# Fixed PSUM banks for queries, score blocks and values in the second attention layer of a two-layer kernel

## The chip, the cores and the metric

The kernel runs on one core of one Trainium2 chip, in one launch. The metric is the device time in microseconds (us) of one execution, as the median of several. A core has five engines that work in parallel, each through its own queue, in order: TensorE (PE in the profile, its weight loads PEld), VectorE (DVE), ScalarE (ACT), GpSimd (POOL) and SyncE (SP), which issues transfers. They meet through semaphores. Matmul results land in PSUM, eight banks of 128 partitions by 512 float32 values, from which only DVE and ACT read.

## What is computed

Two layers on x of shape (8, 512, 128). Layer 1 is windowed attention and a top-1 mixture of experts. Layer 2, in which the change lies, is causal attention with one shared key and value head, and a gated feed-forward:

```python
xn = _layernorm(x, axis=-1)
x = x + _L1_attn_ref(xn, ...) + _L1_ffn_ref(xn, ...)
# _L1_attn_ref: 16 heads of 64, one k and v for all
xn = layernorm(x, g1)
q = xn @ Wq.T
kv = xn @ Wkv.T
k, v = (kv[..., :DIM_HEAD], kv[..., DIM_HEAD:])
q, k = (l2norm(q), l2norm(k))
q, k = (q * srt, k * srt)
sim = jnp.einsum('bhid,bjd->bhij', q, k)
sim = jnp.where(causal_mask, max_neg, sim)
attn = jax.nn.softmax(sim.astype(jnp.float32), axis=-1).astype(sim.dtype)
out = jnp.einsum('bhij,bjd->bhid', attn, v)
out = out @ Wout.T
return layernorm(out, g2)
# _L1_ffn_ref, weights dequantised from integers
h = jax.nn.silu(gate) * up
return jnp.einsum('bsh,dh->bsd', h, wd)
```

## The kernel before

Three stages run one after the other: layer 1's attention, the experts, then layer 2. Layer 2 runs one sequence b of 512 tokens after the other, `attend(b, last)`, seven in a loop and the eighth written out behind it. Each engine has its own `attend`; the order on an engine is the order of the code.

Within a sequence the 16 heads go in eight pairs, n = 0 to 7 (NP = 8). Two heads of 64 fill the 128 rows of the array side by side. For a pair:

- `project_q(n + 2)` on PE multiplies x by a slice of the query weights (ring_d<-wq_sb in the trace). `squares` on ACT squares the result (arena<-ring_d), `q_sums` on DVE sums it per head (q_sum), `q_length` on POOL takes the power (q_len), and `q_unit` on DVE scales, inverts and writes the normalised query into one of two buffers (q_nat_sb, o_n). q_unit frees the bank of the projected query.
- `turn_q(n + 1)` on PE transposes a normalised query. `q_turned` on ACT copies it twice, in full and rounded (arena, then rows), and `q_low` on DVE takes the difference. The semaphore q_lo then lets the scores of that pair go.
- `scores(n)` and `late_scores(n)` on PE form the scores by key block j = 0 to 3, of 512, 384, 256 and 128 queries (the causal mask cuts the rest), for both heads: three matmuls for each, since keys and queries are split in a high and a low part. `exp_of(n, third)` on ACT takes the exponential in three instructions: head 0 blocks 0 and 1, head 1 blocks 0 and 1, and blocks 2 and 3 of both.
- POOL cuts the diagonals (four selects), behind `q_length` of the same pair. `values1(n - 1)` on PE multiplies by v, and DVE's `values_out` copies the result out. Every second pair `sums1` adds the softmax sums of two pairs into the bank gather.

Between them run the three chunks of the feed-forward: `gate_up(c)` on PE (ring_a<-q_rows,w_gu), its emptying on ACT (tanh and a copy, xn_all<-ring_a), and `silu_up(c)` on DVE. Chunk 0 stands ahead of pair 0, chunks 1 and 2 behind the turn of q in pairs 0 and 1.

Seven of the eight banks are held by two rings. Ring D has three single banks (ring_d) and takes in turn projected queries, values, and at the end the feed-forward output and the spread sums. Ring A has two double banks (ring_a) and takes in turn both early thirds of the scores, the late third, the turned query and the gate/up chunks. A fill of a ring waits until its slot's last content was read. Ring R, for the start of the next sequence, uses the same banks as ring A. DVE also prepares the next sequence's rows in pairs 3 to 6.

## Time and profile before

| | |
|---|---|
| median of 3 runs | 1378.53 us (1378.07 to 1380.86) |
| the profiled execution | 1379.98 us, of which the span is 1378.1 us |
| busy in the span | PE 90%, DVE 65%, ACT 49%, POOL 33% |
| mean granted clock of PE | 0.96 |
| layer 2, all eight sequences | about 699 us |

The span goes from the first to the last instruction of one execution. A window's row gives the busy time of each engine in a stretch. In the order of time each row is an instruction or a run of equal ones, with its start, its length, and in brackets how long its engine was idle before it and what released it. The ends of matmuls are modelled and overlap by up to 0.1 us, so from one matmul group to the next it is best to subtract starts.

### The profile page before, as it was taken

The page shows a single profiled execution, that of the slowest core. Times are in us where ns is not written, and L with a number is a line of the kernel's source. Part 1 is how long each engine was busy: PE and PEld are TensorE (multiplying, and loading weights), DVE is VectorE, ACT ScalarE, POOL GpSimd, SP SyncE. Part 2 cuts the span into 40 slices and gives each one's busy share as a digit, 9 for nine tenths or more (in the row PEclk, how much of TensorE's full clock was granted, in tenths as well). Part 3 has the DMA queues.
Part 4 walks back from the last instruction along what each step waited for, and adds up shares of the span by engine and source line. Part 5 has one row for each costly group of instructions (what it writes and reads, how often), then busy time and mean ns, then how long its engine had stood idle before and what let it go on. Part 6 is the DMA issues. An engine that isn't in the chain of part 4 may idle for free.

```text
span 1378.1 us, 27031 instructions
## 1 busy us (share of the span) xinstructions
PE 1233.6 (90%) x8812; PEld 852.6 (62%) x8812; DVE 898.6 (65%) x2474; ACT 679.7 (49%) x1294; POOL 459.6 (33%) x695
## 2 busy tenths in 40 slices
PE   5999999999999958996499898998999989899896
PEld 3656656666566537996356656666576565656655
DVE  6888888888888754442465656556565566655644
ACT  2766667666766622442253543535425354353440
POOL 4221222212222245331263442534426245263340
PEclk9999999999999967998699999999999999999998
DMA  2300100001000052111000000000000000000000
GB/s 75 89 16 17 24 17 21 20 16 24 16 20 21 9 163 71 46 46 32 3 9 2 11 4 8 8 0 11 4 8 8 0 11 4 0 15 0 8 2 8
DMA packets 34597, 29.78 MB, mean 22 GB/s; under 512 B 5984, under 2 KB 27104, under 8 KB 34528
## 3 DMA queue, kind: packets, MB, share of 16 engines
q1 hardware_dynamic: 32224, 24.22, 6.5%
q0 software_dynamic: 2304, 4.72, 1.5%
q8 instruction: 34, 0.56, 0.2%
q14 instruction: 35, 0.29, 0.1%
HBM read 13.72 MB, written 6.82 MB: 15 GB/s over the span
## 4 chain that ended last, share of the span: by engine, by line
PE 34%; issue 9%; ACT 5%; DVE 2%; POOL 2%; POOLq 0%; ACTq 0%; DVEq 0%
PE ring_a L465 13%; PE ring_d L465 12%; PE gather L465 7%; ACT arena L1400 3%; PE ring_a L469 2%; ACT xn_all L1380 1%; POOL q_len L1163 1%; POOL klen L1169 0%; DVE k_rows L1844 0%; DVE arena L1916 0%; ACT k_rows L1339 0%; ACT arena L1372 0%; DVE m_cols L1902 0%; POOL arena L1187 0%; DVE q_rn L1780 0%
## 5 line engine op out<-in xcount | busy, mean ns | idle before, releaser
L1255 ACT ACTIVATE arena<-ring_a 128x384 f32<-128x384 f32 (+1 forms) x512 | 252.6, 550 | 138.9 <-PE ring_a L465 138.8
L1400 ACT ACTIVATE arena<-ring_a 128x896 f32<-128x896 f32 (+1 forms) x192 | 163.2, 884 | 206.9 <-PE ring_a L465 206.8
L1531 DVE CUSTOM_DVE_ANT_0 arena<-ring_d,arena 128x512 bf16<-128x512 f32 (+1 forms) x391 | 231.4, 614 | 37.5 <-PE ring_d L465 31.2
L1027 POOL TENSOR_SCALAR_AFFINE_SELECT arena<-arena 128x512 f32<-128x512 f32 x128 | 81.7, 639 | 357.1 <-ACT arena L1255 357.1
L465 PE MATMUL ring_a<-rows,k_rows 64*128 64x512 f32 (+3 forms) x1536 | 160.5, 343 | 43.8 <-ACT xn_all L1380 26.4
L465 PE MATMUL ring_a<-q_max,rows 128*128 128x384 f32 (+1 forms) x512 | 195.5, 385 | 0.9 <-ACT arena L1255 0.4
L465 PEld LDWEIGHTS ring_a<-rows,k_rows 64*128 64x128 f32 x1536 | 121.1, 192 | 81.4 <-ACT xn_all L1380 29.3
L465 PE MATMUL ring_d<-rows,q_rows 128*128 128x512 f32 (+1 forms) x391 | 161.3, 414 | 5.4 <-DVE mx L1531 3.3
L1163 POOL TENSOR_TENSOR q_len<-q_sum,exponents 128x8 f32<-128x8 f32 x64 | 105.2, 1645 | 182.0 <-DVE q_sum L1820 182.0
L465 PE MATMUL ring_d<-arena,v_aug 128*64 128x512 f32 (+3 forms) x1024 | 150.2, 438 | 0.0
L465 PEld LDWEIGHTS ring_d<-rows,q_rows 128*128 128x128 f32 x391 | 74.7, 191 | 81.5 <-DVE mx L1531 52.7
L465 PE MATMUL ring_a<-arena,v_aug 128*32 128x384 f32 (+1 forms) x1024 | 122.8, 551 | 1.9 <-POOL arena L1027 1.0
L465 PEld LDWEIGHTS ring_d<-arena,v_aug 128*64 128x64 f32 x1024 | 68.0, 136 | 78.9 <-issue 68.5
L1187 POOL TENSOR_SCALAR_AFFINE_SELECT arena<-arena 128x256 f32<-128x256 f32 x256 | 98.1, 413 | 42.9 <-ACT arena L1400 42.9
L1820 DVE TENSOR_REDUCE q_sum<-arena 128x8 f32<-128x512 f32 x64 | 43.7, 683 | 102.6 <-ACT arena L1372 102.6
L465 PEld LDWEIGHTS ring_a<-q_max,rows 128*128 128x128 f32 x512 | 96.3, 189 | 20.6 <-ACT arena L1255 6.2
L1531 DVE CUSTOM_DVE_ANT_0 arena<-gather,arena 128x512 bf16<-128x512 f32 (+1 forms) x121 | 76.5, 632 | 16.6 <-PE gather L465 10.4
L1312 ACT ACTIVATE arena<-ring_a,arena 128x128 f32<-128x128 f32 x160 | 50.1, 364 | 74.8 <-PE ring_a L465 74.8
L1874 DVE COPY arena<-ring_d 128x512 f32<-128x512 f32 x64 | 43.8, 685 | 64.8 <-PE ring_d L465 64.8
L1838 DVE TENSOR_TENSOR rows<-arena,rows 128x512 fp32r<-128x512 f32 x64 | 44.3, 693 | 63.1 <-ACT rows L1388 62.2
L465 PE MATMUL ring_a<-arena 128*128 128x128 f32 x320 | 78.1, 399 | 0.0
L465 PE MATMUL gather<-wout_sb,arena 128*128 128x128 f32 x512 | 68.8, 281 | 8.7 <-DVE arena L1916 8.7
(226 smaller groups left out, 2069.6 us busy)
## 6 DMA issues: line engine op xcount, KB each, us to landing
rows<-k_rows SPq DMA_DIRECT2D x128, 64.0 KB, 2.0
...
arena<-tokens_x,tokens_now POOLq DMA_INDIRECT x40, 2.5
...
```

What stands on the lines that cost most here:

```text
L465: return pe.matmul(out, lhs, rhs, start=start, stop=stop, skip_group_check=True)
L469: return [pe.transpose(slot[:, i * P:(i + 1) * P], tile_of(i), ident[:]) for i in range(n)][-1]
L1027: pool.affine_select(out=v, in_=v, compare_op=ALU.is_ge, fill=0.0, base=0, pattern=[[0, HG], [1 if late else -1, P]], channel_multiplier=- ...
L1163: pool.tensor_tensor(q_len[:, 0:2 * NT], q_sum[:, 0:2 * NT], exponents[:, NT:3 * NT], ALU.pow).then_inc(s["lens"].sem, s["lens"].add(1))
L1187: ins = pool.affine_select(out=v, in_=v, compare_op=ALU.is_ge, fill=0.0, base=0, pattern=[[0, 2], [1, P]], channel_multiplier=-1)
L1255: act.activation(probs[:, t % NT, h, 0:many], A.slot(("cols", c))[:, 0:many], ACT.Exp).then_inc(A.free.sem, A.free.add(1))
L1312: ins = act.activation(hidden[:, u % 2, c], hidden_bank(u, c), ACT.Relu, bias=staged[:, u, AT_B1 + c:AT_B1 + c + 1])
L1400: act.activation(dst, src, ACT.Exp).then_inc(A.free.sem, A.free.add(1))
L1531: dve.tensor_tensor_reduce(dump[:, h % 2, 0:many], M.slot(("max", n))[:, 0:many], masks[:, m, at:at + many], 1.0, LOWEST, ALU.add, ALU.max ...
L1820: dve.reduce_sum(q_sum[:, 0:2 * NT], q_sq, AX.X).then_inc(s["sums"].sem, s["sums"].add(1))
L1838: dve.tensor_tensor(q_lo[:, n % QB, :], q_full, q_hi[:, n % QB, :].bitcast(F32), ALU.subtract).then_inc(s["q_lo"].sem, s["q_lo"].add(1))
L1874: dve.tensor_copy(o1[:, n, :], D.slot(("o", n))[:]).then_inc(D.free.sem, D.free.add(1))
```

## The change

The two rings give way to fixed banks. Q (one bank) holds the projected query. O (one bank) holds values. S (one bank) holds the turned query and half of block 2's scores; the other half goes to O's bank. M (a double bank) holds blocks 1 and 3, W (a double bank) block 0 and the gate/up chunks. At the end of a sequence Z rotates over the banks of Q, S and O, three single banks as ring D did.

All scores of a pair are formed in one go, M, W, S, ahead of the projection. ACT's exponentials follow as M (1024 columns), S (512) and W (1024), 2560 columns in three instructions as before. ACT turns q behind all three and takes the squares behind that. DVE does q_low ahead of q_sums, and values_out ahead of q_unit. The chunks 1 and 2 are formed in pairs 1 and 2, `silu_up(0)` stands first in pair 0. `values1(n)` also waits for S's exponential of pair n + 1, because of the shared bank. The probabilities lie in another order in SBUF, and POOL selects the same four pieces of 256 columns. Amounts and types of the work are the same.

```diff
-        banks_d = [ctx.enter_context(nc.psum_tensor(f"ring_d{n}", [P, T], F32)) for n in range(DR)]
+        pair = ctx.enter_context(nc.psum_tensor("pair", [P, 2 * T], F32))
+        banks_d = [ctx.enter_context(nc.psum_tensor("ring_d0", [P, T], F32))[:], pair[:, T:2 * T], pair[:, 0:T]]
         gather = ctx.enter_context(nc.psum_tensor("gather", [P, T], F32))
         banks_a = [ctx.enter_context(nc.psum_tensor(f"ring_a{n}", [P, 2 * T], F32)) for n in range(AR)]
...
-            s["D"] = Ring(s["d_full"], s["d_free"], banks_d)
-            s["A"] = Ring(s["a_full"], s["a_free"], banks_a)
+            s["Q"], s["O"] = Ring(s["q_full"], s["q_free"], banks_d[0:1]), Ring(s["o_full"], s["o_free"], banks_d[1:2])
+            s["S"] = Ring(s["s_full"], s["s_free"], banks_d[2:3])
+            s["M"], s["W"] = Ring(s["m_full"], s["m_free"], banks_a[1:2]), Ring(s["w_full"], s["w_free"], banks_a[0:1])
+            s["Z"] = Ring(s["e_full"], s["e_free"], [banks_d[n] for n in (0, 2, 1)])
...
                 def project_q(n):
-                    pe.wait_ge(D.free.sem, D.fillable(b, ("q", n)))
-                    q_of(n, D.slot(("q", n))).then_inc(D.full.sem, D.full.add(1))
+                    pe.wait_ge(Q.free.sem, Q.fillable(b, ("q", n)))
+                    q_of(n, Q.slot(("q", n))).then_inc(Q.full.sem, Q.full.add(1))
 
...
                 def scores(n):
+
                     pe.wait_ge(s["q_lo"].sem, s["q_lo"].at(b, n + 1))
-                    for c in range(2):
-                        pe.wait_ge(A.free.sem, A.fillable(b, ("probs", n, c)))
-                    sl = [A.slot(("probs", n, c)) for c in range(2)]
-                    side_by_side([sl[c][:, 0:512] for c in range(2)], 0, n, 0)
-                    for ins in side_by_side([sl[c][:, 512:896] for c in range(2)], 1, n, 128):
-                        ins.then_inc(A.full.sem, A.full.add(1))
-
-                def late_scores(n):
-                    pe.wait_ge(A.free.sem, A.fillable(b, ("probs", n, 2)))
-                    sl = A.slot(("probs", n, 2))
-                    side_by_side([sl[:, c * T:c * T + 256] for c in range(2)], 2, n, 256)
-                    side_by_side([sl[:, c * T + 256:c * T + 384] for c in range(2)], 3, n, 384)[-1].then_inc(A.full.sem, A.full.add(1))
+                    pe.wait_ge(M.free.sem, M.fillable(b, ("probs", n, 0)))
+                    sl = M.slot(("probs", n, 0))
+                    side_by_side([sl[:, c * T:c * T + 384] for c in range(2)], 1, n)
+                    side_by_side([sl[:, c * T + 384:c * T + 512] for c in range(2)], 3, n).then_inc(M.full.sem, M.full.add(1))
+                    pe.wait_ge(W.free.sem, W.fillable(b, ("probs", n, 2)))
+                    sl = W.slot(("probs", n, 2))
+                    side_by_side([sl[:, c * T:c * T + 512] for c in range(2)], 0, n).then_inc(W.full.sem, W.full.add(1))
+                    pe.wait_ge(S.free.sem, S.fillable(b, ("probs", n, 1)))
+                    if n > 1:
+                        pe.wait_ge(O.free.sem, O.emptied(b, ("o", n - 2)))
+                    side_by_side([bank[:, 0:256] for bank in (S.slot(("probs", n, 1)), banks_d[1])], 2, n)                         .then_inc(S.full.sem, S.full.add(1))
 
...
                 def values1(n):
                     pe.wait_ge(s["masked"].sem, s["masked"].at(b, 3 * (n + 1)))
-                    pe.wait_ge(D.free.sem, D.fillable(b, ("o", n)))
-                    sl = D.slot(("o", n))
+                    pe.wait_ge(S.free.sem, S.emptied(b, ("probs", min(n + 1, NP - 1), 1)))
+                    pe.wait_ge(O.free.sem, O.fillable(b, ("o", n)))
+                    sl = O.slot(("o", n))
                     [mm(sl[D1 * c:D1 * c + D1, j * P:T], v1[:, j, :], p_of(n, c, j), start=(j == 0), stop=(j == NT - 1))
-                     for j in range(NT) for c in range(2)][-1].then_inc(D.full.sem, D.full.add(1))
+                     for j in range(NT) for c in range(2)][-1].then_inc(O.full.sem, O.full.add(1))
```

```diff
                     scores(n)
                     if n + 2 < NP:
                         project_q(n + 2)
-                    late_scores(n)
                     if n + 1 < NP:
                         turn_q(n + 1)
-                    if n < 2:
-                        gate_up(n + 1)
+                    if 0 < n < HC:
+                        gate_up(n)
                     if n:
                         values1(n - 1)
                         if n % 2 == 0:
...
+                pe.wait_ge(Q.free.sem, Q.emptied(b, ("q", NP - 1)))
+                pe.wait_ge(Z.free.sem, Z.fillable(b, "ffn"))
...
+                    if n == 0:
+                        pe.wait_ge(S.free.sem, S.emptied(b, ("probs", NP - 1, 1)))
+                    if n == 1:
+                        pe.wait_ge(O.free.sem, O.emptied(b, ("o", NP - 1)))
+                    pe.wait_ge(Z.free.sem, Z.fillable(b, ("1/sum", n)))
+                    mm(Z.slot(("1/sum", n))[:], spread[:, n, :], rsum_rows).then_inc(Z.full.sem, Z.full.add(1))
...
                 for n in range(NP):
                     if n + 2 < NP:
                         q_length(s, n + 1, b)
-                    at = (n % PB) * 2560
-                    for third, spans in enumerate((((0, 512),), ((896, 512),), ((1792, 256), (2176, 256)))):
-                        pool.wait_ge(s["A"].free.sem, s["A"].emptied(b, ("probs", n, third)))
+                    p = probs1[:, n % PB]
+                    for third, ring in enumerate((s["M"], s["S"], s["W"])):
+                        pool.wait_ge(ring.free.sem, ring.emptied(b, ("probs", n, third)))
                         apart(pool)
-                        for lo, gap in spans:
-                            v = arena[:, at + lo:at + lo + 2 * gap].rearrange("p (j t) -> p j t", j=2)[:, :, 0:P]
+                        if third == 0:
+                            diagonals = [p[:, 512:1536].rearrange("p (c t) -> p c t", c=2)[:, :, at:at + P] for at in (0, 384)]
+                        else:
+                            at, many = (None, (0, 512), (1536, 1024))[third]
+                            diagonals = [p[:, at:at + many].rearrange("p (c t) -> p c t", c=2)[:, :, 0:P]]
+                        for v in diagonals:
                             ins = pool.affine_select(out=v, in_=v, compare_op=ALU.is_ge, fill=0.0, base=0,
                                                      pattern=[[0, 2], [1, P]], channel_multiplier=-1)
                         ins.then_inc(s["masked"].sem, s["masked"].add(1))
...
                 gate_up(0)
                 for n in range(NP):
-                    exp_of(n, 0)
-                    exp_of(n, 1)
+                    for third in range(3):
+                        exp_of(n, third)
+                    if n + 1 < NP:
+                        q_turned(n + 1)
                     if n + 2 < NP:
                         squares(n + 2)
-                    exp_of(n, 2)
-                    if n + 1 < NP:
-                        q_turned(n + 1)
-                    if n < 2:
-                        gate_up(n + 1)
+                    if 0 < n < HC:
+                        gate_up(n)
...
                 for n in range(NP):
+                    if n == 0:
+                        silu_up(0)
+                    if n + 1 < NP:
+                        dve.wait_ge(S.free.sem, S.emptied(b, ("q.T", n + 1)))
+                        q_low(n + 1)
                     if n + 2 < NP:
                         q_sums(s, n + 1, b)
-                    if n + 1 < NP:
-                        dve.wait_ge(A.free.sem, A.emptied(b, ("q.T", n + 1)))
-                        q_low(n + 1)
+                    if n:
+                        values_out(n - 1)
                     if n + 2 < NP:
                         q_unit(s, n + 2, b)
-                    if n < 3:
+                    if 0 < n < HC:
                         silu_up(n)
-                    if n:
-                        values_out(n - 1)
```


PE in pair 3, up to the turn of q 4, as the last sequence has it. Before (ring_a is ring A, ring_d ring D, C_a_free and C_d_free say that they were read; o_n or q_nat_sb is the normalised query):

```order
L465 MATMUL ring_a<-rows,k_rows 128x512 [waits C_a_free,C_q_lo]
L465 MATMUL ring_a<-rows,k_rows 128x512 x5
L465 MATMUL ring_a<-rows,k_rows 128x384 x6
L465 MATMUL ring_d<-wq_sb,o_raw 128x128 [waits C_d_free]
L465 MATMUL ring_d<-wq_sb,o_raw 128x128 x3
L465 MATMUL ring_a<-rows,k_rows 128x256 [waits C_a_free]
L465 MATMUL ring_a<-rows,k_rows 128x256 x5
L465 MATMUL ring_a<-rows,k_rows 128x128 x6
L469 MATMUL ring_a<-ident,q_nat_sb 128x128 [waits C_a_free,C_d_free]
L469 MATMUL ring_a<-ident,q_nat_sb 128x128 x3
```

And now (ring_d is Q, pair is S and O, ring_a is M and then W):

```order
L469 MATMUL ring_a<-rows,k_rows 128x384 [waits C_m_free,C_q_lo]
L469 MATMUL ring_a<-rows,k_rows 128x384 x5
L469 MATMUL ring_a<-rows,k_rows 128x128 x6
L469 MATMUL ring_a<-rows,k_rows 128x512 [waits C_w_free]
L469 MATMUL ring_a<-rows,k_rows 128x512 x5
L469 MATMUL pair<-rows,k_rows 128x256 [waits C_o_free,C_s_free]
L469 MATMUL pair<-rows,k_rows 128x256 x5
L469 MATMUL ring_d<-wq_sb,o_raw 128x128 [waits C_q_free]
L469 MATMUL ring_d<-wq_sb,o_raw 128x128 x3
L473 MATMUL pair<-ident,q_nat_sb 128x128 [waits C_s_free,C_q_free]
L473 MATMUL pair<-ident,q_nat_sb 128x128 x3
```

The late scores moved ahead of the projection, the projection waits for Q's only bank, and S's scores wait for O and S.

ACT in the same pair. Before: early exponentials, squares of q 5, late exponential, two copies of the turned q 4.

```order
L1400 ACTIVATE arena<-ring_a 128x896 [waits C_pv,C_a_full]
L1400 ACTIVATE arena<-ring_a 128x896 [waits C_a_full]
L1372 ACTIVATE arena<-ring_d 128x512 [waits C_sums,C_d_full]
L1400 ACTIVATE arena<-ring_a 128x768 [waits C_a_full]
L1387 ACTIVATE arena<-ring_a 128x512 [waits C_q_lo,C_a_full]
L1388 ACTIVATE rows<-ring_a 128x512
```

And now:

```order
L1415 ACTIVATE arena<-ring_a 128x1024 [waits C_pv,C_m_full]
L1415 ACTIVATE arena<-pair 128x512 [waits C_s_full]
L1415 ACTIVATE arena<-ring_a 128x1024 [waits C_w_full]
L1402 ACTIVATE arena<-pair 128x512 [waits C_q_lo,C_s_full]
L1403 ACTIVATE rows<-pair 128x512
L1387 ACTIVATE arena<-ring_d 128x512 [waits C_sums,C_q_full]
```

The squares (arena<-ring_d) moved from the third place to the last, behind the copies.

DVE in the same pair, before:

```order
L1820 TENSOR_REDUCE q_sum<-arena 128x8 [waits C_squared]
L1838 TENSOR_TENSOR rows<-arena,rows 128x512 [waits C_a_free]
L1778 TENSOR_SCALAR q_len<-q_len 128x8 [waits C_lens]
L1780 RECIPROCAL q_rn<-q_len 128x8 [waits C_own]
L1830 SCALAR_TENSOR_TENSOR o_n<-ring_d,q_rn 128x512 [waits C_a_full,C_own]
L1874 COPY arena<-ring_d 128x512 [waits C_d_full]
```

And now:

```order
L1852 TENSOR_TENSOR rows<-arena,rows 128x512 [waits C_s_free]
L1834 TENSOR_REDUCE q_sum<-arena 128x8 [waits C_squared]
L1888 COPY arena<-pair 128x512 [waits C_o_full]
L1792 TENSOR_SCALAR q_len<-q_len 128x8 [waits C_lens]
L1794 RECIPROCAL q_rn<-q_len 128x8 [waits C_own]
L1844 SCALAR_TENSOR_TENSOR o_n<-ring_d,q_rn 128x512 [waits C_s_full,C_own]
```

The low part (rows<-arena,rows) moved ahead of the sums, and the copy of the values ahead of the scaling of the query.

## Rows read from the trace of the kernel before

**Rows 1.** The page, part 1: busy us (share of the span) xinstructions of TensorE.
```profile
PE 1233.6 (90%) x8812; PEld 852.6 (62%) x8812; DVE 898.6 (65%) x2474; ACT 679.7 (49%) x1294; POOL 459.6 (33%) x695
```

**Rows 2.** Windows, one per sequence: us, busy us (xcount) by engine, PEclk, DMA, GB/s.
```profile
939.72:1024.90 85.18, 77.31 (x672) 53.26 (x673) 52.61 (x115) 38.26 (x60) 35.40 (x52) 1.00 0.02 6
1024.90:1112.63 87.73, 80.24 (x672) 55.71 (x673) 52.52 (x115) 38.60 (x60) 35.55 (x52) 0.96 0.02 6
...
sum 698.64, PE 628.02 PEld 433.33 DVE 408.56 ACT 303.74 POOL 271.94; mean PE 78.50 PEld 54.17 DVE 51.07 ACT 37.97 POOL 33.99
```

**Rows 3.** Order of time, TensorE, opening: start us, us, engine line op tiles xcount [idle].
```profile
939.72 1.20 PE L465 MATMUL ring_a<-q_rows,w_gu 128*128 128x512 f32 x4 [0.16 <-DVE k_rows L1844]
942.60 1.49 PE L465 MATMUL ring_a<-rows,k_rows 64*128 64x512 f32 x12 [1.68 <-ACT xn_all L1380]
944.01 1.16 PE L465 MATMUL ring_d<-wq_sb,o_raw 128*128 128x128 f32 x8
...
947.17 1.20 PE L465 MATMUL ring_a<-q_rows,w_gu 128*128 128x512 f32 x4 [0.51 <-ACT arena L1400]
949.97 1.51 PE L465 MATMUL ring_a<-rows,k_rows 64*128 64x512 f32 x12 [1.60 <-ACT xn_all L1380]
951.41 1.16 PE L465 MATMUL ring_d<-wq_sb,o_raw 128*128 128x128 f32 x8
```

**Rows 4.** Order of time, TensorE, middle and end of the same sequence.
```profile
959.33 1.16 PE L465 MATMUL ring_d<-wq_sb,o_raw 128*128 128x128 f32 x8
...
967.85 1.16 PE L465 MATMUL ring_d<-wq_sb,o_raw 128*128 128x128 f32 x8
...
970.35 2.38 PE L465 MATMUL ring_d<-arena,v_aug 128*64 128x512 f32 x16
...
974.21 1.16 PE L465 MATMUL ring_d<-wq_sb,o_raw 128*128 128x128 f32 x8
...
982.82 1.16 PE L465 MATMUL ring_d<-wq_sb,o_raw 128*128 128x128 f32 x8
...
991.17 0.66 PE L469 MATMUL ring_a<-ident,o_n 128*128 128x128 f32 x4
...
996.35 1.48 PE L465 MATMUL ring_a<-rows,k_rows 64*128 64x512 f32 x12
998.83 0.91 PE L465 MATMUL ring_a<-rows,k_rows 64*128 64x256 f32 x12 [1.00 <-ACT arena L1400]
999.67 4.53 PE L465 MATMUL ring_d<-arena,v_aug 128*64 128x512 f32 x32
1004.13 0.66 PE L469 MATMUL ring_a<-ident,xn_all 128*128 128x128 f32 x4
```

**Rows 5.** Order of time, all engines, pair 3: the way of one query pair.
```profile
970.20 0.69 DVE L1820 TENSOR_REDUCE q_sum<-arena 128x8 f32<-128x512 f32 x1 [2.69 <-ACT arena L1372]
...
970.73 0.63 ACT L1387 ACTIVATE arena<-ring_a 128x512 f32<-128x512 f32 x1
...
970.97 1.67 POOL L1163 TENSOR_TENSOR q_len<-q_sum,exponents 128x8 f32<-128x8 f32 x1 [2.64 <-DVE q_sum L1820]
971.21 0.64 ACT L1388 ACTIVATE rows<-ring_a 128x512 fp32r<-128x512 f32 x1
...
971.88 0.69 DVE L1838 TENSOR_TENSOR rows<-arena,rows 128x512 fp32r<-128x512 f32 x1 [0.99 <-ACT rows L1388]
...
972.63 1.48 POOL L1187 TENSOR_SCALAR_AFFINE_SELECT arena<-arena 128x256 f32<-128x256 f32 x4
...
973.41 0.69 DVE L1830 SCALAR_TENSOR_TENSOR o_n<-ring_d,q_rn 128x512 f32<-128x512 f32 x1
```

**Rows 6.** Order of time, all engines, opening of the same sequence.
```profile
941.03 0.69 DVE L1838 TENSOR_TENSOR rows<-arena,rows 128x512 fp32r<-128x512 f32 x1
...
941.53 1.02 ACT L1380 ACTIVATE xn_all<-ring_a 128x1024 f32<-128x1024 f32 x1
...
945.20 0.69 DVE L1934 TENSOR_TENSOR o_t<-xn_all,fulls 128x512 f32<-128x512 f32 x1
```

114 lines of the change are left out of this document (57 added, 57 removed).

## The prediction

> **What bounds the kernel now.** I read the page first: TensorE (PE) is busy 90% of the span [rows 1], so what matters is when PE waits. Then the windows of layer 2: it runs eight almost identical sequences of about 86 us, half of the span, and nothing outside them is touched but the address of some banks. In a sequence at full clock PE is busy 77.31 of 85.18 us; one with a granted clock of 0.96 takes 87.73 [rows 2]. The reader is to see there that a sequence has about 8 us of PE idle time and that a low clock costs 0 to 2.5 us; the mean busy time, 78.50 against 77.31, puts the clock's part at 1.2 us a sequence, 9.5 us in all. Last comes the order of time of PE in one clean sequence, the one from 939.72 to 1024.90 us. It opens with waits of 1.68, 0.51 and 1.60 us for ScalarE (ACT), which has to empty the gate/up chunk (xn_all) before ring A can be filled again [rows 3]. In its middle PE is full: from one query projection (ring_d<-wq_sb) to the next it takes 6.36 us (967.85 to 974.21) in a pair without sums and 8.61 (974.21 to 982.82) with them. At the end the late scores of pairs 6 and 7 wait about 1.0 us each for an exp [rows 4] (one of the two is shown).
>
> I cut the stretch from gate/up chunk 0 (939.72) to the turn of the next sequence's x (1004.13), 64.41 us, at the query projections and rebuild each piece. Behind 1004.13 the order is unchanged but for ring names.
>
> **Part 1, work on PE: nothing is saved.** The same matmuls run. Scores cost 1.41 us for the early and 0.84 for the late part, 2.25 in all, now in one go; a projection is 1.1 us, a turn of q 0.6, a gate/up chunk 1.15, values of a pair 2.3, sums of two pairs 2.3 [rows 3, 4]. Split by columns I take the first block (M) as 0.95, W as 0.8, S as 0.5, worked out from 2.25. The exp total on ACT stays near 2.6 us a pair. Chunks 1 and 2 move one pair later: a piece between projections loses 1.15 us and another gains it.
>
> **Part 2, what goes.** The waits of 1.68, 0.51 and 1.60 us at the opening, the one of about 0.5 before chunk 2, and the two of 1.0 at the end: 6.3 us. Each has a successor.
>
> **Part 3, the opening.** M no longer shares a bank with chunk 0, but it needs the low part of q 0, which VectorE (DVE) finishes at 941.03 + 0.69 [rows 6]; with 0.1 us to PE that is 2.1 us after the start, and PE idles 0.97. M ends at 3.05; chunk 0 is emptied at 942.55, 2.83 after the start, so W does not wait. The first projection starts at 2.1 + 2.25 = 4.35 (before 4.29: no gain, since now the late scores stand ahead of it).
>
> **Part 4, the new chain, the main term.** The projected q now has one bank (Q). Projection n+3 can't start until DVE has normalised q n+2 out of it; before it had its own turn in a ring of three. And the squares of q n+2 now stand on ACT behind the copies of turned q n+1, where they stood ahead of the last exp. The chain from one projection to the next: projection 1.1, turn of the other q 0.65, to ACT 0.05, first copy 0.48 (970.73 to 971.21), then the second copy. That starts at 2.3. The squares follow 0.48 behind it and take 0.6; DVE does the low part first (0.69 from 971.88) and then q's sums, which end about 2.0 after the second copy's start; POOL's power is 0.08 later and takes 1.67; DVE's scale, reciprocal and normalisation end 1.46 after that (972.64 to 974.10); 0.1 to PE [rows 5]. Sum: 2.3 + 2.0 + 0.08 + 1.67 + 1.46 + 0.1 = 7.6 us. Each piece is the larger of this chain and PE's own work.
>
> Piece by piece, in us, before [rows 3, 4] and after:
> - start to projection of q 2: 4.29, now 4.35.
> - q 2 to q 3: 7.40. PE's own work is now 1.1 + 0.6 + 2.25, with a wait for the low part of q 1. DVE has two silu instructions of chunk 0 ahead of that low part, behind the output sum that ends at 945.89 [rows 6]; they end at 947.3, some 0.2 later than the copies allow. So the chain gives 7.8.
> - q 3 to q 4 (959.33): 7.92. Work 1.1 + 0.6 + 1.15 + 2.3 + 2.25 = 7.4; chain 7.6.
> - q 4 to q 5: 8.52, now with chunk 2: 9.67, work longer than the chain.
> - q 5 to q 6: 6.36. Chain: 7.6. This is the cleanest place: 1.2 us of new idle time.
> - q 6 to q 7: 8.61, work, unchanged.
> - q 7 to the turn of q 7 (991.17): 8.35 with the old wait for an exp. Pair 6 projects nothing, but its turn needs q 7 normalised, the same chain: 7.6.
> - turn to the scores of pair 7 (996.35): 5.18, unchanged; the low part of q 7 is ready 2.7 behind the turn.
> - scores of pair 7 to the turn of x: 7.78. Now scores 2.25; values 6 share the S and O banks and wait for exp S, 0.05 + 0.6 + 0.05 = 0.7; values 2.3; **values 7 need O's only bank**, so they wait for DVE's copy of values 6: 0.69, the size of the low part [rows 5], + 0.15 = 0.85; values 2.3. Sum 8.4.
>
> After: 4.35 + 7.8 + 7.6 + 9.67 + 7.6 + 8.61 + 7.6 + 5.18 + 8.4 = 66.8 us, against 64.4: 2.4 us longer, and with the small gaps that the rounded work leaves out 2.5. Times eight: 20 us.
>
> **What the rest is hidden by.** M's exp, 1.02 us for 1024 columns [rows 6], ends before S's scores do. The turn of q shares S's bank: S's exp ends 0.65 behind the scores, the projection covers 1.1. The wait for O before the S scores: values end as the next pair begins, DVE copies by 1.0, S comes at 1.75. Gate/up 1 and 2 are emptied 4.8 us behind a projection and W is written again at 6.0 or later. POOL's four selects (1.48 us [rows 5]) stand behind its power and now wait with it, yet end about 7.6 behind a projection, and values need them at 9.3; the two gathers that POOL issues in pairs 1 and 2 come behind the selects. Were that cover of 1.7 us gone, each late microsecond would come in full, 6 times a sequence. DVE's work on the next sequence's rows stands behind the normalisation of q and in front of the next low part, where 2 to 3 us are free.
>
> [...] The trace shows the query banks refilled in turn, each at a time when the last projection's chain is nowhere near them. [...]
>
> **Rivals.** (A) *The other side: the chain hides.* If it took under 6.4 us, no projection would wait. Pieces: q 2 to q 3 falls to 6.2 (the low part of q 1), q 3 to q 4 to 7.5, q 5 to q 6 to 6.4, q 7 to its turn to 7.0 (S's exp), 3.5 us less: 63.4 us, 1.0 faster than before, 1371 in all. For it: six waits do go. Against it: 1.2 us of 7.6 would have to vanish, and every link is a measured row. It decides at 6.4 us. (B) *More low clock.* New idle time sits close together (0.97, about 2.3 and 1.6 us within 13 us), and the sequences that lose clock now lose it there. Doubling its cost adds 9.5 us: 1408. [...] (C) *Less low clock*: a low clock falls partly into the chain's slack or does not occur; at most 9.5 us less: 1389. (D) *The change is neutral*: the chain is 0.8 us shorter and the last wait hides; 1378.
>
> **How the numbers follow.** Profiled execution 1379.98 us (span 1378.1); with 20 us, 1400.0. That execution stands 1.45 above the median of the runs, 1378.53, so against the median: 1398.5. Chances: forecast 0.60 (own range 1392 to 1404), B 0.17, C 0.11, A 0.08, D 0.04. The chain's bounds are 7.3 (sums not behind the low part, short latencies) and 7.9 (POOL's power at 1.7 and 0.1 for each hand-over), over four pieces and eight sequences 10 us either way; the split of the scores does not move the sum. So the range is 1386 to 1412. Within 0.2% (2.8 us), about what this kernel's runs can tell from no change, lie D and a little of A: faster 0.07, same 0.05, slower 0.88.
>
> **What would show it.** Right: sequences of about 87.7 us where the clock is full; a wait of PE before ring_d<-wq_sb of 1.2 us in every second pair, ended by DVE's normalisation; about 1.5 before q 3; no wait of scores for xn_all; 0.85 between the values of pairs 6 and 7. Wrong: projections without a wait (A), or PE waiting for POOL's masks before the values, which would make it far slower.

## The result and the profile after

The changed kernel takes 1388.46 us as a median against 1378.30 in the same comparison: a ratio of 1.0073, 95% interval 1.0055 to 1.0090. So it is slower, as forecast, by 10 us and not by 20. The profiled execution takes 1388.47 us, its span 1386.6.

The page, part 1, and the windows of the changed kernel, one per sequence (us, busy us by engine, granted clock, DMA share, GB/s); the last window is the eighth sequence with its tail.

```profile
PE 1218.9 (88%) x8812; PEld 858.5 (62%) x8812; DVE 897.5 (65%) x2474; ACT 688.0 (50%) x1294; POOL 455.0 (33%) x695
```

```profile
854.84:943.38 88.54, 77.65 (x672) 55.50 (x673) 52.37 (x115) 39.55 (x60) 34.67 (x52) 0.96 0.02 6
943.38:1029.85 86.47, 74.91 (x673) 53.55 (x673) 52.53 (x115) 39.45 (x60) 34.98 (x52) 1.00 0.02 6
1029.85:1118.01 88.16, 78.06 (x672) 56.13 (x673) 52.37 (x115) 39.44 (x60) 35.00 (x52) 0.96 0.02 6
...
sum 615.36, PE 541.06 PEld 387.33 DVE 363.30 ACT 276.87 POOL 242.14; mean PE 77.29 PEld 55.33 DVE 51.90 ACT 39.55 POOL 34.59
```

```profile
1294.93:1386.60 91.67, 71.85 (x632) 50.61 (x632) 44.25 (x86) 35.35 (x51) 24.34 (x42) 0.95 0.02 7
```

At full clock a sequence takes 86.47 us, where the kernel before took 85.18 [rows 2]: 1.29 longer, in seven sequences 9.0. The seven take 615.36 us, 10.1 more than seven times 86.47; those of before took 604.87, 8.6 more than seven times 85.18. So in these seven a low clock costs 1.5 us more than before. The eighth is 2.1 shorter (91.67 against 93.73). Together 8.4, and the spans differ by 8.5. TensorE (PE) is busy for 74.91 us of the clean sequence, before for 77.31 [rows 2]: less busy time for the same matmuls, and more idle time.

The shorter eighth sequence is luck of the clock for the most part. Its opening, from chunk 0 to the gate/up chunk in pair 1, before and after:

```profile
1284.37:1301.77 17.40, 13.37 (x80) 10.45 (x80) 9.20 (x23) 10.39 (x16) 5.75 (x8) 0.80 0.05 16
```

```profile
1294.93:1308.43 13.50, 8.43 (x76) 7.17 (x77) 8.46 (x22) 8.35 (x12) 4.72 (x7) 1.00 0.07 21
```

In the clean sequence of before (from 939.72) that stretch takes 14.75 us, so about 2.7 us of the 17.40 go with the granted clock of 0.80. Over all eight sequences the changed kernel thus lost about 1 us less to the clock than the kernel before, not more.

The order of time on PE in that sequence (start, length, engine, line, operation, tiles, count, idle time before and its releaser); L469 has the matmuls and L473 the transposes, ring_d is Q, pair is S and O, ring_a is M and W.

```profile
943.38 1.18 PE L469 MATMUL ring_a<-q_rows,w_gu 128*128 128x512 f32 x4 [0.16 <-DVE k_rows L1858]
945.52 1.84 PE L469 MATMUL ring_a<-rows,k_rows 64*128 64x384 f32 x18 [0.95 <-DVE rows L1852]
...
947.64 1.16 PE L469 MATMUL ring_d<-wq_sb,o_raw 128*128 128x128 f32 x8
...
952.14 1.82 PE L469 MATMUL ring_a<-rows,k_rows 64*128 64x384 f32 x18 [2.91 <-DVE rows L1852]
...
955.90 1.16 PE L469 MATMUL ring_d<-wq_sb,o_raw 128*128 128x128 f32 x8 [1.59 <-DVE q_nat_sb L1844]
...
963.24 1.16 PE L469 MATMUL ring_d<-wq_sb,o_raw 128*128 128x128 f32 x8 [0.39 <-DVE o_n L1844]
...
972.41 1.16 PE L469 MATMUL ring_d<-wq_sb,o_raw 128*128 128x128 f32 x8
...
979.79 1.16 PE L469 MATMUL ring_d<-wq_sb,o_raw 128*128 128x128 f32 x8 [1.36 <-DVE o_n L1844]
...
985.91 1.84 PE L469 MATMUL ring_a<-rows,k_rows 64*128 64x384 f32 x18
987.59 0.53 PE L469 MATMUL pair<-rows,k_rows 64*128 64x256 f32 x6
988.04 1.16 PE L469 MATMUL ring_d<-wq_sb,o_raw 128*128 128x128 f32 x8
989.04 0.60 PE L473 MATMUL pair<-ident,q_nat_sb 128*128 128x128 f32 x4
989.57 2.37 PE L469 MATMUL pair<-arena,v_aug 128*64 128x512 f32 x16
...
995.45 0.65 PE L473 MATMUL pair<-ident,o_n 128*128 128x128 f32 x4 [1.38 <-DVE o_n L1844]
...
1000.62 1.84 PE L469 MATMUL ring_a<-rows,k_rows 64*128 64x384 f32 x18
...
1003.50 2.38 PE L469 MATMUL pair<-arena,v_aug 128*64 128x512 f32 x16 [0.69 <-ACT arena L1415]
1006.76 2.37 PE L469 MATMUL pair<-arena,v_aug 128*64 128x512 f32 x16 [0.89 <-DVE arena L1888]
1009.07 0.66 PE L473 MATMUL ring_a<-ident,xn_all 128*128 128x128 f32 x4
```

The old waits [rows 3, 4] are gone. In their place stand those of the forecast: for the low part of q (0.95 and 2.91, where the forecast had 0.97 and about 2.3), for the normalisation before a projection (1.59, 0.39, 1.36) and before the turn of q 7 (1.38), and at the end for the exp (0.69) and for the copy of the values (0.89). The pieces, in us:

| piece | before | forecast | after |
|---|---|---|---|
| start to q 2 | 4.29 | 4.35 | 4.26 |
| q 2 to q 3 | 7.40 | 7.8 | 8.26 |
| q 3 to q 4 | 7.92 | 7.6 | 7.34 |
| q 4 to q 5 | 8.52 | 9.67 | 9.17 |
| q 5 to q 6 | 6.36 | 7.6 | 7.38 |
| q 6 to q 7 | 8.61 | 8.61 | 8.25 |
| q 7 to its turn | 8.35 | 7.6 | 7.41 |
| turn to scores 7 | 5.18 | 5.18 | 5.17 |
| scores 7 to the turn of x | 7.78 | 8.4 | 8.45 |
| sum | 64.41 | 66.8 (66.9 with gaps) | 65.69 |

### The profile page after: what moved, and what is told of

The parts are those of the page before. It is cut to its first block, busy times and chain, and to the rows that moved or that the text cites. A ratio compares the mean times of both kernels' runs of the same rounds, so it can differ in the third digit from the quotient of the medians.

```text
span 1386.6 us, 27028 instructions
## 1 busy us (share of the span) xinstructions
PE 1218.9 (88%) x8812; PEld 858.5 (62%) x8812; DVE 897.5 (65%) x2474; ACT 688.0 (50%) x1294; POOL 455.0 (33%) x695
## 4 chain that ended last, share of the span: by engine, by line
issue 27%; PE 20%; POOL 12%; DVE 5%; ACT 1%; POOLq 1%; DMA 0%; DVEq 0%; ACTq 0%
PE ring_a L469 8%; PE gather L469 6%; PE pair L469 4%; POOL arena L1202 4%; POOL q_len L1174 3%; POOL arena L1168 2%; POOL v_aug L1068 1%; DVE stats L1454 1%; POOL rstd L1009 1%; ACT arena L1415 1%; PE ring_a L473 1%; PE pair L473 1%; DVE q_len L1792 1%; POOL veps L1007 0%; DVE mv L1459 0%
## 5 line engine op out<-in xcount | busy, mean ns | idle before, releaser
L1415 ACT ACTIVATE arena<-ring_a 128x1024 f32<-128x1024 f32 x128 | 130.8, 1022 | 158.9 <-PE ring_a L469 158.9
L469 PE MATMUL ring_a<-q_max,rows 128*128 128x384 f32 (+1 forms) x512 | 195.6, 386 | 0.9 <-ACT arena L1270 0.5
L1545 DVE CUSTOM_DVE_ANT_0 arena<-pair,arena 128x384 bf16<-128x384 f32 (+1 forms) x271 | 162.4, 614 | 26.0 <-PE pair L469 22.9
L469 PE MATMUL pair<-arena,v_aug 128*64 128x512 f32 (+3 forms) x1024 | 152.0, 439 | 12.6 <-DVE arena L1888 7.1
L469 PE MATMUL ring_a<-rows,k_rows 64*128 64x384 f32 (+2 forms) x1152 | 120.4, 350 | 28.8 <-DVE rows L1852 27.8
L469 PEld LDWEIGHTS pair<-arena,v_aug 128*64 128x64 f32 x1024 | 69.7, 137 | 95.4 <-issue 77.7
L469 PE MATMUL ring_a<-arena,v_aug 128*32 128x384 f32 (+1 forms) x1024 | 122.7, 551 | 1.9 <-POOL arena L1038 1.0
L469 PEld LDWEIGHTS ring_a<-rows,k_rows 64*128 64x128 f32 x1152 | 88.0, 189 | 46.4 <-DVE rows L1852 24.0
L469 PE MATMUL pair<-rows,q_rows 128*128 128x384 f32 (+1 forms) x271 | 111.4, 413 | 2.4 <-DMA rows<-k_rows 1.8
L469 PEld LDWEIGHTS ring_a<-q_max,rows 128*128 128x128 f32 x512 | 96.3, 189 | 20.6 <-ACT arena L1270 6.2
L1888 DVE COPY arena<-pair 128x512 f32<-128x512 f32 x64 | 44.0, 687 | 79.8 <-PE pair L469 79.1
L469 PEld LDWEIGHTS pair<-rows,q_rows 128*128 128x128 f32 x271 | 52.2, 193 | 55.3 <-DVE mx L1545 34.2
L1545 DVE CUSTOM_DVE_ANT_0 arena<-ring_d,arena 128x384 bf16<-128x384 f32 (+1 forms) x120 | 73.6, 613 | 11.6 <-PE ring_d L469 8.5
L469 PE MATMUL ring_d<-wq_sb,o_raw 128*128 128x128 f32 x384 | 60.2, 304 | 21.2 <-DVE o_n L1844 11.7
L469 PE MATMUL ring_a<-arena 128*128 128x128 f32 x320 | 78.0, 399 | 0.0
```

Source lines behind the costliest of these rows:

```text
L469: return pe.matmul(out, lhs, rhs, start=start, stop=stop, skip_group_check=True)
L1415: act.activation(dst, src, ACT.Exp).then_inc(ring.free.sem, ring.free.add(1))
L1545: dve.tensor_tensor_reduce(dump[:, h % 2, 0:many], M.slot(("max", n))[:, 0:many], masks[:, m, at:at + many], 1.0, LOWEST, ALU.add, ALU.max ...
L1888: dve.tensor_copy(o1[:, n, :], O.slot(("o", n))[:]).then_inc(O.free.sem, O.free.add(1))
```

## The experiments

Ratios are to the kernel before, timed on the same chip; the changed kernel has 1.0073. A clean sequence is one whose granted clock shows as 1.00. The changed kernel was timed in the first comparison only, and the kernel before had medians from 1374.35 to 1378.30 us in the five comparisons, so a difference between the ratios of two runs is good to about 4 us; lengths of clean sequences are far closer than that.

### Is it the chain through the query's one bank?

The power on GpSimd (POOL) is one link of it. It was doubled in the changed kernel and in the kernel before, by the same edit:

```diff
+                if s is SC:
+                    pool.tensor_tensor(q_len[:, 2 * NT:4 * NT], q_sum[:, 0:2 * NT], exponents[:, NT:3 * NT], ALU.pow)
                 pool.tensor_tensor(q_len[:, 0:2 * NT], q_sum[:, 0:2 * NT], exponents[:, NT:3 * NT],
                                    ALU.pow).then_inc(s["lens"].sem, s["lens"].add(1))
```

> The changed kernel, in which GpSimd takes each power of a query pair's sums twice, the first time into columns that nobody reads: 1.65 us more between VectorE's sums and the normalisation. Theory of the chain: q 2 to q 3, q 3 to q 4, q 5 to q 6 and q 7 to its turn grow by 1.65 each, q 6 to q 7 from its own work of 8.25 to 9.03, q 4 to q 5 by nothing (9.17 of work); 7.4 us a sequence, +59 us in eight: ratio to the kernel before about 1.050. If the cuts of the diagonals, behind the power on GpSimd, now come late for the values as well, some us more. Rival (the projected query's single bank is not what TensorE waits for): under +15, ratio below 1.018.

Measured: 1465.68 us in one execution, ratio 1.065. PE in the changed kernel with the doubled power, sequence from 1070.60, before projection 6:

```profile
1111.85 1.16 PE L469 MATMUL ring_d<-wq_sb,o_raw 128*128 128x128 f32 x8 [2.99 <-DVE o_n L1846]
```

The wait of 1.36 has become 2.99, 1.63 more, about the length of one power (1.67 in the trace). The pieces of that sequence grew by 1.61, 1.59, 0, 1.63, 0.69 and 1.61, as expected. Against the changed kernel that is +79 us, of which these pieces make 57; the rest goes with the clock: no sequence shows 1.00, six of the first seven show 0.90 to 0.92.

> The same doubling of the power in the kernel before, with its ring of three banks. Theory: the chain of a query has until the turn in the next pair; in the trace of before, the normalisation of q 5 ends at 974.10 and its turn starts at 976.21, 2.1 us later, so 1.65 us more are hidden in the middle; at the opening, where pairs come closer, up to 1 us a sequence may show: 0 to +8 us, ratio 1.000 to 1.006. Rival (a power on GpSimd costs the same in both kernels, banks or not): ratio 1.04 or more.

Measured: 1389.96 us in one execution, ratio 1.010, a little over the expected range. The clean sequence is 86.25 us, 1.08 longer than before, from one new wait, at the turn of q 7 in pair 6, where no projection stands between scores and turn:

```profile
1086.84 0.65 PE L469 MATMUL ring_a<-ident,o_n 128*128 128x128 f32 x4 [0.99 <-DVE o_n L1832]
```

The same 1.65 us cost 13 us in the kernel with three banks and 79 in the one with a single bank. That the chain of the projected query bounds the changed kernel is shown. That the wait before a projection is the bank's follows from the code, in which `project_q` waits for nothing but the bank (C_q_free). The wait before the turn of q 7 (1.38) is not the bank's: that turn reads the normalised query itself. How much is due to the single bank and how much to the later place of the squares no run separates, since none gave the query a second bank.

The chain can also be shortened. A first try put ScalarE (ACT) and VectorE (DVE) back to the order of before:

```diff
 # ACT
-                    for third in range(3):
-                        exp_of(n, third)
-                    if n + 1 < NP:
-                        q_turned(n + 1)
+                    exp_of(n, 0)
+                    exp_of(n, 1)
                     if n + 2 < NP:
                         squares(n + 2)
+                    exp_of(n, 2)
+                    if n + 1 < NP:
+                        q_turned(n + 1)
 # DVE: q_sums(s, n + 1, b) ahead of q_low(n + 1)
```

> The changed kernel (1388.5) with two orders put back: ScalarE takes the squares ahead of the exp of block 0, and VectorE takes q's sums ahead of q_low. Banks, waits and amounts of work are those of the changed kernel. Theory of the chain: the single bank of the projected query sets the time between projections (7.38 us in the trace of the changed kernel, where TensorE's own work is about 6.0), and most of that chain is where the squares stand. With the squares ahead, sums end about 2.5 behind the projection's start, the power at 4.2, q_low slips in and delays the normalisation to 6.1 or 6.2. So the waits before projections 4 and 6 (0.39 and 1.36) and before the turn of q 7 (1.38) go to about 0.2 each: -2.6 us a sequence, the wait of scores 1 for q_low 1 (2.91) grows by 0.2 at most: -21 us, about 1367, sequences of 83.9 us where the clock is full. Rival (the banks themselves or the joined scores cost the time, wherever the squares stand): 1385 to 1389.

Measured: 1396.11 us, ratio 1.0164 (1.0147 to 1.0181): slower still. That expectation was wrong. PE in the sequence from 944.41:

```profile
960.33 1.20 PE L469 MATMUL ring_a<-q_rows,w_gu 128*128 128x512 f32 x4 [1.17 <-ACT arena L1415]
...
980.95 1.81 PE L469 MATMUL ring_a<-rows,k_rows 64*128 64x384 f32 x18 [0.57 <-DVE rows L1853]
```

The piece from q 5 to q 6 did fall, to 6.55. But ACT waits for the projection before the squares, the exp of block 0 stands behind them, and its bank W is what chunks 1 and 2 need: 1.17 us of new wait, twice a sequence. And q_low comes late: 0.57 here, and the wait of 2.91 grew to 3.5. The new waits outweigh the old ones: the piece from q 4 to q 5 grew by 1.43, to 10.60, and none of the six sequences behind the first is clean. With the squares one place later, behind the exp of block 0, and pair 0 left alone, W is emptied in time:

```diff
 # ACT, behind the three exps
+                    if 1 <= n < NP - 2:
+                        squares(n + 2)
                     if n + 1 < NP:
                         q_turned(n + 1)
-                    if n + 2 < NP:
+                    if n < 1:
                         squares(n + 2)
 # DVE: q_sums ahead of q_low for the same n
```

> The changed kernel with the squares between the exp of block 0 and the copies of the turned q, and VectorE's sums ahead of q_low, in pairs 1 to 5. Pair 0 stays as changed, so q_low 1 is not delayed, and block 0's bank is emptied as early as in the changed kernel, so chunks 1 and 2 should not wait (both went wrong in the run with the squares ahead of the exp of block 0). Theory of the chain: the squares end 2.3 behind the projection's start, the power ends at 4.8, and the normalisation, behind q_low, at 6.25, against 7.38. The piece from q 5 to q 6 falls from 7.38 to 6.4, q 3 to q 4 from 7.34 to 7.0 (its own work), q 7 to its turn by 0.7 (then the exp of block 2 holds it): -2.0 us a sequence, -16 us against the changed kernel, ratio to the kernel before 0.995 or 0.996. Rival (waits only move, as they did in the run before: q_low comes late for the next scores, and the clock falls as often or oftener): ratio 1.005 to 1.012.

Measured: 1370.12 us, ratio 0.9948 (0.9932 to 0.9964). PE in the sequence from 1105.70, q 5 to q 6:

```profile
1134.77 1.16 PE L469 MATMUL ring_d<-wq_sb,o_raw 128*128 128x128 f32 x8
...
1140.87 1.16 PE L469 MATMUL ring_d<-wq_sb,o_raw 128*128 128x128 f32 x8
```

6.10 us without a wait, against 7.38. With these orders alone the fixed banks are faster than the rings.

### Why are TensorE's own groups shorter than the sum took them?

```diff
 # PE, in scores(n), between block 0 and block 2
+                    if n + 2 < NP:
+                        project_q(n + 2)
                     pe.wait_ge(S.free.sem, S.fillable(b, ("probs", n, 1)))
...
                     scores(n)
-                    if n + 2 < NP:
-                        project_q(n + 2)
```

> The changed kernel with the projection of q between the scores of block 0 and those of block 2, as the projection stood between early and late scores in the kernel before. It is for the length of TensorE's own groups. Before, from a projection to the scores behind it took 1.09 us, and scores in two parts took 2.25; changed, from a projection to the turn behind it takes 0.99 and the scores in one go 2.13. Theory of alternation: each step between matmuls of 64 rows side by side and matmuls of 128 rows costs some 0.1 us, so here the projection takes 1.09 again up to the scores, and the scores of all four blocks 2.2 to 2.25. Rival (the difference comes from the banks, or from how ends are modelled): 0.99 and 2.13 stay. The time itself: the turn of q has to wait for the exp of block 2, which now ends 2.2 behind the projection's start and not 1.0, so the chain grows by 1.2 to 8.6 us: +1.2 in four pieces and +0.4 in one, 8 sequences, about +40: 1428.

Measured: 1475.66 us in one execution, ratio 1.074, where 1428 us was expected: the chain grew as expected (q 5 to q 6 8.9 us), and the clock fell in every sequence (0.90 to 0.93), which I had not counted. For the lengths, PE in pair 3 of the sequence from 978.66:

```profile
1011.62 1.83 PE L469 MATMUL ring_a<-rows,k_rows 64*128 64x384 f32 x18
1013.38 1.16 PE L469 MATMUL ring_d<-wq_sb,o_raw 128*128 128x128 f32 x8
1014.47 0.62 PE L469 MATMUL pair<-rows,k_rows 64*128 64x256 f32 x6
```

Blocks M and W take 1.76 us up to the projection, and in the changed kernel, where scores follow them, 1.68 (985.91 to 987.59). The projection takes 1.09 up to the scores, and 1.00 up to a turn (988.04 to 989.04). So each step between matmuls that use 64 rows side by side (64*128 in the rows) and matmuls of the full array costs 0.08 to 0.09 us, with the banks unchanged. The change takes two such steps out of each pair that has a projection, six of the eight.

### The opening and the end of a sequence

```diff
 # DVE
-                    if n == 0:
-                        silu_up(0)
...
-                    if 0 < n < HC:
+                    if n < HC:
                         silu_up(n)
```

> The changed kernel with VectorE's silu of chunk 0 behind the normalisation of q 2 again, as in the kernel before, where the change put it first in pair 0. In the changed kernel's trace ScalarE's copies of the turned q 1 end at 950.44, but q_low 1 starts at 951.41, behind the two silu instructions (950.07 and 950.80). Theory: q_low 1 comes 0.9 us earlier, the wait of the scores of pair 1 (2.91) falls to 2.0, the normalisation of q 2 also comes 0.9 earlier, and the piece from q 2 to q 3 falls from 8.26 to 7.4: -0.9 us a sequence, -7 us: ratio to the kernel before 1.002. Rival (the chain from the squares on holds q 3, and q_low 1 only moves the wait): ratio 1.006 to 1.008.

Measured: 1375.38 us, ratio 0.9988 (0.9969 to 1.0008); a clean sequence is 85.52 us, 0.95 less. The four DVE rows of the changed kernel that it is about:

```profile
948.86 0.69 DVE L1950 TENSOR_TENSOR o_t<-xn_all,fulls 128x512 f32<-128x512 f32 x1
950.07 0.69 DVE L1880 SCALAR_TENSOR_TENSOR fulls<-xn_all 128x512 f32<-128x512 f32 x1 [0.52 <-DVE o_t L1950]
950.80 0.69 DVE L1883 SCALAR_TENSOR_TENSOR v_aug<-fulls,xn_all 128x512 f32<-128x512 f32 x1
951.41 0.68 DVE L1852 TENSOR_TENSOR rows<-arena,rows 128x512 fp32r<-128x512 f32 x1
```

and with silu late, DVE's q_low 1 and PE's scores of pair 1:

```profile
946.14 0.69 DVE L1852 TENSOR_TENSOR rows<-arena,rows 128x512 fp32r<-128x512 f32 x1 [0.91 <-ACT rows L1403]
...
946.88 1.84 PE L469 MATMUL ring_a<-rows,k_rows 64*128 64x384 f32 x18 [1.98 <-DVE rows L1852]
```

The wait fell from 2.91 to 1.98, and the piece from q 2 to q 3 from 8.26 to 7.34. By the ratios the time fell by 12 us, not 7; eight clean sequences account for 7.6, and the other 4 are put down to the clock, with five of six sequences at 1.00 where the changed kernel has one (below).

```diff
 # PE, values1(n): pair 6 into Q's bank; DVE copies from there
+                    if n == NP - 2:
+                        pe.wait_ge(Q.free.sem, Q.emptied(b, ("q", NP - 1)))
+                        sl = banks_d[0]
+                    else:
...
```

> The changed kernel with the values of pair 6 written to Q's bank, which is idle by then, and read from there. That takes away the wait for the exp of block 2 before values 6 (0.69 us in the changed kernel's trace) and the wait for VectorE's copy before values 7 (0.89). Theory (the last piece's part of the sum): -1.58 us a sequence, 8 sequences, -12.6: about 1376. Rival, the wait is handed on: values 7 begin 1.6 us earlier, about 4.5 behind the start of scores 7, and GpSimd's last cut of pair 7 comes at about the same time, so up to 0.4 comes back: 1379. Rival, the end is set elsewhere (VectorE's way to the spread sums): 1385 to 1388.

Measured: 1369.00 us, ratio 0.9964 (0.9949 to 0.9979). The clean sequence is 84.89 us, 1.58 less: both waits are gone. By the ratios that is 15 us less, where 12.6 were expected.

```profile
1166.92 2.37 PE L469 MATMUL ring_d<-arena,v_aug 128*64 128x512 f32 x16
1169.38 2.37 PE L469 MATMUL pair<-arena,v_aug 128*64 128x512 f32 x16
```

```diff
 # PE and ACT
-                    if 0 < n < HC:
-                        gate_up(n)
+                    if n < 2:
+                        gate_up(n + 1)
```

> The changed kernel with the gate/up chunks 1 and 2 in pairs 0 and 1 again, on TensorE and ScalarE, as the kernel before had them. Chunk 1 then falls into the wait of 2.91 us before the scores of pair 1, which falls to about 1.6, and the piece from q 4 to q 5 loses a chunk: 9.17 to 7.9. Theory without the clock: -1.3 us a sequence, about 1378. Theory with the clock: in five of the eight sequences of the changed kernel the matmuls behind that wait of 2.91 run at half clock (the chunk of pair 1 comes 2.6 us behind the projection and not 1.36) and lose about 2 us; if it is the length of the wait that throws the clock back, a wait of 1.6 leaves it up, another -10 us: about 1368. Rival: the scores of block 0 in pair 1 now wait for ScalarE to empty chunk 1, and the gain is lost there: 1385 to 1390.

Measured: 1372.94 us, ratio 0.9990 (0.9980 to 1.0000). A clean sequence is 85.5 us, 0.95 less and not 1.3, since the scores of pair 1 still wait 1.63; and five of six sequences are clean. By the ratios the time fell by 11 us: 7.6 for the shorter sequences and about 4 more, where the theory with the clock had 10 more.

### The clock

Of the six sequences behind the first, so many show a granted clock of 1.00, beside the longest wait of PE in the opening:

| kernel | longest wait, us | at 1.00 |
|---|---|---|
| before | 1.68 | 2 of 6 |
| changed | 2.91 | 1 |
| squares early | 3.5 | 0 |
| values in Q | 2.91 | 2 |
| squares third | 2.91 | 0 |
| chunks early | 1.63 | 5 |
| silu late | 1.98 | 5 |
| values in Q and chunks early | 1.64 | 3 |
| and squares third | 1.63 | 5 |
| and silu late | 1.28 | 5 |
| projection between the scores | 1.98 | 0 |
| power twice, changed | 2.9 | 0 |
| power twice, before | 1.68 | 1 |

In the five sequences of the changed kernel at 0.96 the clock is low right behind the wait of 2.91. Windows of the sequence from 1029.85, the wait, the 8 us behind it, and what follows:

```profile
1035.64:1038.62 2.98, 0.07 (x2) 0.00 (x2) 2.43 (x5) 1.66 (x4) 0.00 (x0) 1.00 0.28 88
1038.62:1046.62 8.00, 7.55 (x41) 6.42 (x41) 1.87 (x5) 3.73 (x6) 3.21 (x6) 0.57 0.00 0
1046.62:1060.00 13.38, 13.30 (x123) 8.41 (x124) 8.82 (x16) 7.74 (x12) 9.89 (x13) 1.00 0.04 10
```

In the middle stretch, at 0.57 in all, the granted clock is 0.86 in the first microsecond, 0.50 over the next six and 0.73 in the last:

```profile
1038.62:1039.62 1.00, 1.00 (x12) 1.00 (x14) 0.54 (x1) 0.00 (x0) 0.38 (x1) 0.86 0.00 0
1039.62:1045.62 6.00, 5.55 (x30) 4.88 (x29) 1.25 (x3) 2.73 (x4) 2.83 (x6) 0.50 0.00 0
1045.62:1046.62 1.00, 1.00 (x5) 0.54 (x3) 0.08 (x1) 1.00 (x3) 0.00 (x0) 0.73 0.00 0
```

The longest wait is not the whole of it, though. In the run with the projection between the scores no wait of the opening is above 1.98, and yet the clock falls in every sequence, here behind waits of 1.98, 1.93 and 0.69 us within 9 us:

```profile
990.66:999.66 9.00, 7.61 (x30) 4.26 (x32) 1.93 (x3) 4.60 (x7) 2.94 (x6) 0.64 0.00 0
```

To tell cause from company in the changed kernel, the wait was filled with work that nobody needs:

```diff
+                    if n == 0:
+                        pe.wait_ge(M.free.sem, M.emptied(b, ("probs", 0, 0)))
+                        for _ in range(8):
+                            mm(M.slot(("probs", 0, 0))[:, 0:T], w_gu[:, 0, 0:P], x_hi, start=True, stop=True)
```

> The changed kernel with eight extra matmuls of 128x512 on TensorE behind the turn of q 1, written to block 1's bank and overwritten by the scores of pair 1 right after; nobody reads them. They fill about 2.3 of the 2.91 us for which TensorE waits there for q_low 1, and hold nobody else up. It is for the clock: of 24 sequences (the first left out) in four kernels in which that wait is 2.9 us or longer, 3 show a mean granted clock of 1.00; of 30 in five kernels in which it is 2.0 or shorter, 23 do. Theory (the long idle time brings the low clock): five or six of the six sequences at 1.00, and where the clock is full a sequence stays at 86.5: -8 to -10 us for all, ratio to the kernel before 1.000. Rival (the low clock comes with the change and the shorter waits only happened to go with it): at most two of six at 1.00, ratio 1.006 to 1.009.

Measured: 1378.14 us, ratio 1.0008 (0.9993 to 1.0023): 9 us less with more work. (The 23 of 30 in the expectation leave out the kernel before, which has 2 of 6 with a longest wait of 1.68.) All six sequences show 1.00, at the same length as the changed kernel's clean one. One of them, and PE in it:

```profile
1025.35:1111.82 86.47, 76.77 (x680) 54.85 (x681) 52.55 (x115) 39.48 (x60) 35.06 (x52) 1.00 0.02 6
```

```profile
1030.96 2.11 PE L469 MATMUL ring_a<-q_rows,w_gu 128*128 128x512 f32 x8
1034.12 1.84 PE L469 MATMUL ring_a<-rows,k_rows 64*128 64x384 f32 x18 [1.06 <-DVE rows L1856]
```

So in the changed kernel the wait of 2.91 us brings the low clock in nearly all sequences (one of the six stayed clean with it), and the low clock costs it about 9 us. Waits of up to 2 us left it up in 23 of 30 sequences of five kernels, but in 2 of 6 of the kernel before, 1 of 6 of the same with the power twice and none of the run with the projection between. Why the kernel before, with waits of at most 1.68, is clean in only two of six stays open: its three waits [rows 3] stand within 10 us, but so do three in the run with silu late (0.95, 1.98, 1.57), which is clean in five.

### All together

> The changed kernel with both the values of pair 6 in Q's bank and the chunks 1 and 2 in pairs 0 and 1. Alone they gave 1.58 and 0.95 us in a sequence at full clock, and the second left the clock up in all but one sequence. If they add: 83.9 us a sequence at full clock, -12.6 and -11.5 us against the changed kernel, ratio to the kernel before 0.990. Rival (the clock, which stayed up in three or four sequences of the first and in seven of the second, falls more often again when waits go): 0.993 to 0.996.

Measured: 1361.98 us, ratio 0.9896 (0.9871 to 0.9920), 84.0 us a clean sequence; the two add.

> Values of pair 6 in Q's bank, chunks 1 and 2 in pairs 0 and 1, and the squares third in pairs 1 to 5, together. The first two gave a ratio of 0.9896, and the squares alone 16 or 18 us: 82.0 us a sequence at full clock, ratio to the kernel before 0.977 or 0.978. If chunk 2, now ahead of the squares' new place on the next pair, or the clock, takes something back: 0.981 to 0.985.

Measured: 1340.01 us, ratio 0.9741 (0.9710 to 0.9772), 81.6 us.

> The same with the silu of chunk 0 late as well. If all four add: 81.1 us a sequence at full clock, ratio to the kernel before 0.971 to 0.973. Rival: in pair 0 chunk 1 now has to be emptied by ScalarE, which waits for the silu of chunk 0 for its buffer, so a later silu holds block 0's bank and the scores of pair 1: 0.976 to 0.978, no better than without.

Measured: 1334.48 us, ratio 0.9685 (0.9662 to 0.9709), 80.7 us, five of six sequences at 1.00. Both beat their expectations by 0.3 points. In the last, a clean sequence and two of its remaining waits, the longest, before q 3, and the one before the turn of q 7:

```profile
926.79:1007.48 80.69, 75.37 (x672) 53.73 (x673) 52.84 (x115) 39.09 (x60) 35.58 (x52) 1.00 0.02 7
```

```profile
938.40 1.16 PE L469 MATMUL ring_d<-wq_sb,o_raw 128*128 128x128 f32 x8 [1.28 <-DVE q_nat_sb L1851]
...
974.67 0.66 PE L473 MATMUL pair<-ident,o_n 128*128 128x128 f32 x4 [0.69 <-ACT arena L1420]
```

The fixed banks are thus no mistake: with the orders mended they are 3% faster than the two rings. No run changed the orders in the kernel with the rings, so it is not shown that fixed banks are the better choice.

## Why the prediction was wrong in size

The direction was right, and each successor wait is in its place; 1388.5 lies within the range but 10 us below the forecast. In the profiled executions the kernel is 8.5 us longer and not 20, 11.5 off. A clean sequence grew by 1.29 us and not by 2.5: 8.5 us of the error in seven sequences. The eighth came out 2.1 shorter and not 2.5 longer, 4.6 us, of which 2.7 are luck of the clock; and the low clock in the seven took 1.5 back. The steps, in the prediction's own terms and for a sequence at full clock:

- **Part 1, "work on PE: nothing is saved", is the step that failed: the term was mis-sized.** I took a turn as 0.6, a projection as 1.1 and the scores as 2.25 in all, lengths that were read where scores stand around the projection. In the new order they are 0.53, 1.00 and 2.13. The three pieces that are pure work came out 0.09, 0.50 and 0.36 shorter: 0.95 a sequence, 7.6 us, the largest part of the error. The matmuls are the same, but their order saves time. Of the 0.36 from q 6 to q 7, two steps between tile shapes make 0.17, and the run with the projection between the scores brought these back, 0.08 and 0.09 in the two groups that it moved. Another 0.07 was a short wait inside the 8.61 of before (the late scores start there 1.16 behind the projection, elsewhere 1.09). The other 0.12 no run took apart. From q 4 to q 5 turn and chunk together take 1.45 (964.24 to 965.69), where I had 0.6 and 1.15: a turn with a chunk behind it takes 0.35.
- **Part 4, the chain, was right and 0.2 us too long.** Q 5 to q 6 was forecast at 7.6 and took 7.38. ACT's and DVE's rows, pair 3, from the projection at 972.41:

```profile
975.09 0.60 ACT L1387 ACTIVATE arena<-ring_d 128x512 f32<-128x512 f32 x1
975.24 0.69 DVE L1852 TENSOR_TENSOR rows<-arena,rows 128x512 fp32r<-128x512 f32 x1 [3.34 <-ACT rows L1403]
975.85 0.68 DVE L1834 TENSOR_REDUCE q_sum<-arena 128x8 f32<-128x512 f32 x1
...
976.61 1.67 POOL L1174 TENSOR_TENSOR q_len<-q_sum,exponents 128x8 f32<-128x8 f32 x1 [3.29 <-DVE q_sum L1834]
...
979.05 0.69 DVE L1844 SCALAR_TENSOR_TENSOR o_n<-ring_d,q_rn 128x512 f32<-128x512 f32 x1
```

  The sums end 4.1 behind the projection, forecast 4.3, since projection and turn ahead of them are shorter; the rest is as forecast within 0.05. Three pieces, 0.67 a sequence, -5.4 us.
- **Part 4, q 2 to q 3, was 0.46 too short**, +3.7 us. The silu does not start when the output sum ends (949.55) but at 950.07, and with the silu late the piece fell by 0.92. I had no row for a DVE instruction that follows the end of a sequence.
- **Part 3, the opening, and the end** (4.35 against 4.26, 8.4 against 8.45) were right, and so was the cover of the masks: PE never waits for POOL there.
- **The rivals.** A, the chain hides, is refuted by the doubled power. C, a lower cost of the clock, gave 1389 and so the right time for a wrong reason: over the eight sequences the clock cost about 1 us less than before, not 9.5. B had the mechanism, a long new wait that brings the clock down (2.91 us: one of six sequences at 1.00, six of six with the wait filled), at a small net size, because the clean clock was already lost in most sequences before. I had priced B's wait, but the rows I had show full clock through 1.68 and 1.60 us [rows 2, 3]; a wait of 2.9 was outside what they could tell.
- **Not every refill of a single bank costs time.** In four of the six pieces behind a projection the normalisation holds PE (1.59, 0.39, 1.36, 1.38), in the last of them not through the bank; in the other two (9.17 and 8.25 of work against a chain of 7.38) it costs nothing.
